# Attention and feed-forward layer in float32: maxima products moved into the middle of the background blocks

## What is computed

```python
scores = jnp.einsum('bhqd,bhkd->bhqk', Q, K) / np.sqrt(HD)
w = jax.nn.softmax(scores, axis=-1)
attn = jnp.einsum('bhqk,bhkd->bhqd', w, V)
x = _layernorm(x + (out @ Wo.T + bo))
g = jnp.einsum('th,ih->ti', xf, gate_w) * gate_s
u = jnp.einsum('th,ih->ti', xf, up_w) * up_s
out = jnp.einsum('ti,hi->th', jax.nn.silu(g) * u, down_w) * down_s
x = _layernorm(x + out)
```

## Time and profile before

| what | value |
|---|---|
| runs, median (lowest to highest) | 1011.74 us (1010.34 to 1012.72), 3 runs |
| profiled execution, device time | 1010.08 us |
| its span in the trace | 1008.1 us |
| PE, DVE, ACT busy | 99%, 80%, 64% of the span |
| granted TensorE clock | 0.998 |

### The profile page before, as it was taken

One profiled execution on the slowest core, in us unless ns is written; L12 is line 12 of the kernel. 1 busy time (PEld: TensorE's weight loads), 2 busy tenths in 40 slices (PEclk: granted clock), 3 DMA queues, 4 the chain that ended last, 5 costly groups with the idle time before them and its releaser, 6 DMA issues.

```text
span 1008.1 us, 17487 instructions
## 1 busy us (share of the span) xinstructions
PE 993.2 (99%) x6698; PEld 546.0 (54%) x6698; DVE 803.6 (80%) x1376; ACT 647.6 (64%) x1223; POOL 274.4 (27%) x284
## 2 busy tenths in 40 slices
PE   9999999999999999999999999999999999999996
PEld 4643435445434344443444444444368888888885
DVE  7999797998797999789899999999622666463635
ACT  5179796887787888788666688888852420322221
POOL 4361040241255540257210153565001001000002
PEclk9999999999999999999999999999999999999999
DMA  7174417234225531534140457331439113331011
GB/s 250 54 206 123 116 51 205 76 89 86 56 81 139 83 91 38 95 100 102 35 82 13 123 152 192 72 123 53 159 108 212 59 42 68 59 68 15 1 43 44
DMA packets 64297, 94.92 MB, mean 94 GB/s; under 512 B 37521, under 2 KB 37777, under 8 KB 62129
## 3 DMA queue, kind: packets, MB, share of 16 engines
q1 hardware_dynamic: 63920, 93.49, 36.5%
q10 hardware_dynamic: 288, 0.26, 0.1%
HBM read 53.88 MB, written 27.00 MB: 80 GB/s over the span
## 4 chain that ended last, share of the span: by engine, by line
PE 80%; DVE 15%; ACT 4%; issue 1%; DMA 1%; POOL 0%; DVEq 0%; POOLq 0%
PE PV L499 19%; PE PS L480 18%; PE PSA L570 16%; DVE nmx L1006 13%; PE PSA L458 6%; PE PS L587 6%; PE PS L402 4%; ACT Bn L802 3%; PE PS L526 2%; PE PSA L526 2%; PE PV L587 2%; PE PSA L402 1%; DVE nmx L1010 1%; PE PS L439 1%; DMA A<-in_wqk 1%
## 5 line engine op out<-in xcount | busy, mean ns | idle before, releaser
L1006 DVE TENSOR_REDUCE nmx<-PSA 128x1 f32<-128x512 f32 x976 | 592.6, 680 | 33.1 <-PE PSA L458 32.8
L802 ACT ACTIVATE Bn<-PS 128x512 f32<-128x512 f32 x898 | 476.5, 603 | 79.6 <-PE PS L480 72.5
L458 PE MATMUL PSA<-Kt,Qt 48*128 48x512 f32 x1010 | 359.7, 444 | 0.5 <-DVE nmx L1010 0.4
L480 PE MATMUL PS<-Qt,Kt 50*128 50x512 f32 x1006 | 341.8, 435 | 3.5 <-ACT Bn L802 3.0
L499 PE MATMUL PV<-Bn 128*32 128x256 f32 (+1 forms) x2696 | 298.0, 468 | 0.0
L480 PEld LDWEIGHTS PS<-Qt,Kt 50*128 50x128 f32 x1006 | 164.4, 184 | 240.8 <-ACT Bn L802 183.5
L458 PEld LDWEIGHTS PSA<-Kt,Qt 48*128 48x128 f32 x1010 | 165.7, 184 | 14.5 <-DVE nmx L1006 4.0
L570 PE MATMUL PSA<-x1Th,wr 128*128 128x512 f32 x344 | 135.3, 393 | 0.0
L570 PE MATMUL PSA<-x1Tl,wr 128*128 128x512 f32 x344 | 134.3, 390 | 0.0
L499 PE MATMUL PV<-P,Bn 128*32 128x512 f32 (+1 forms) x320 | 122.9, 466 | 0.0
L837 ACT ACTIVATE sg<-PSA,gs 128x512 f32<-128x512 f32 x43 | 29.6, 690 | 127.8 <-PE PSA L570 127.8
(11 more groups left out here) (177 smaller groups left out, 979.2 us busy)
## 6 DMA issues: line engine op xcount, KB each, us to landing
Qt<-pscr SPq DMA_DIRECT2D x90, 128.0 KB, 5.3
A<-in_wf SPq DMA_DIRECT2D x11, 768.0 KB, 5.5
wr<-A SPq DMA_DIRECT2D x33, 256.0 KB, 4.0
pscr<-A SPq DMA_DIRECT2D x16, 512.0 KB, 3.7
vscr<-Bn SPq DMA_DIRECT2D x32, 256.0 KB, 3.5
Kt<-pscr SPq DMA_DIRECT2D x90, 64.0 KB, 2.8
A<-A SPq DMA_DIRECT2D x16, 256.0 KB, 3.7
Bn<-vscr SPq DMA_DIRECT2D x8, 512.0 KB
```

Source lines behind the costliest of these rows:

```text
L458: op = e.matmul(slot_pair(s)[:, h, :], Qt[n % 3][p:p + NC_, g % 2, 128 * qt:128 * qt + 128], Kt[n % 3][p:p + NC_, 512 * h:512 * h + 512], ...
L480: e.matmul(score_tile(i), Kt[n % 3][rows, 128 * kt:128 * kt + 128], Qt[n % 3][rows, g % 2, 512 * qh:512 * qh + 512], start=True, stop=True ...
L802: e.activation(Pb[p_index(c)], score_tile(score_bank[c]), ACT.Exp, scale=0.25).then_inc(*act_exp.next(c))
L1006: e.tensor_reduce(col, slot_pair(s)[:, h, :], AX.X, ALU.max, negate=True).then_inc(*dve_max[s].next((k, 0) if h == 0 else k))
```

## The change

Four halves of the maxima stream (`AHEAD = 4`, two steps) are issued between the two banks of each of the 11 background blocks. In the four odd units behind a block, u + 1, u + 3, u + 5 and u + 7 (`paid_back`), the half behind the score g = 2 is left out, so that the stream is where it was at u + 8. On DVE, the units whose block has DVE work (42, 162, 170, 178, 186: `with_vector`) have two more `maximum` ahead of `first_norm`, `add_values` and `add_rows`, and units u + 3 and u + 7 behind them have one fewer (`taken_early`). In projection blocks DVE's order is as before. The total of products and reduces is unchanged.

```diff
--- before.py
+++ after.py
@@ -279,6 +279,11 @@
             ffn_at.setdefault(divmod((181, 184, 189, 192, 204, 205, 207, 209, 221, 223, 228)[i], 16), []).append(i)
             low_at.setdefault(divmod(180 + 8 * (1, 1, 2, 3, 4, 4, 5, 5, 6, 6, 7)[i], 16), []).append(i)
         before_flag = 508
+        AHEAD = 4
+        blocks = [16 * n + v for n, v in (*project_at, values_at, *out_at)]
+        paid_back = {b + 1 + 2 * i for b in blocks for i in range(AHEAD)}
+        with_vector = [16 * n + v for n, v in (values_at, *out_at)]
+        taken_early = {b + 4 * i + 3 for b in with_vector for i in range(AHEAD // 2)}
 
         crosswise = (0, 2, 1, 3)
 
@@ -501,8 +506,8 @@
                 if half != 0:
                     op.then_inc(*pe_pv.next(u))
 
-            def out_project(x, b, t2, banks, frees):
-                for j in range(2):
+            def out_project(x, b, t2, banks, frees, rows=(0, 1)):
+                for j in rows:
                     t = 2 * t2 + j
                     ps = banks[j]
                     clear(frees[j])
@@ -703,12 +708,19 @@
                 if at_u in project_at:
                     for h, i in enumerate(pair):
                         project_half(project_at[at_u], h, i, (0, 1, 2, 3))
+                        if h == 0:
+                            advance(AHEAD)
                 if at_u == values_at:
                     for t in range(8):
                         value_rows(1, t, pair[t // 4])
+                        if t == 3:
+                            advance(AHEAD)
                 if at_u in out_at:
                     t2 = out_at[at_u]
-                    out_project(False, 0, t2, [bank(i) for i in pair], [bank_free[i] for i in pair])
+                    for j, i in enumerate(pair):
+                        out_project(False, 0, t2, [bank(i) for i in pair], [bank_free[i] for i in pair], (j,))
+                        if j == 0:
+                            advance(AHEAD)
                     for j, i in enumerate(pair):
                         bank_free[i] = dve_y.at((False, 0, 2 * t2 + j))
 
@@ -716,7 +728,8 @@
                 at_u = divmod(u, 16)
                 for g in range(4):
                     scores(u, g)
-                    advance(1)
+                    if g != 2 or u not in paid_back:
+                        advance(1)
                     if g == 1:
                         background(u)
                     if u % 2 and u >= 2 and g == 0:
@@ -1278,7 +1291,10 @@
             for u in range(SPLIT):
                 at_u = divmod(u, 16)
                 maximum(next(steps))
-                k = next(steps)
+                if u in with_vector:
+                    maximum(next(steps))
+                    maximum(next(steps))
+                k = next(steps) if u not in taken_early else None
                 if at_u in norm_at:
                     first_norm(False, 0, norm_at[at_u])
                 if at_u == values_at:
@@ -1286,7 +1302,8 @@
                         add_values(1, h, i)
                 if at_u in out_at:
                     add_rows(False, 0, out_at[at_u], [bank(i) for i in free_banks(u)])
-                maximum(k)
+                if k is not None:
+                    maximum(k)
                 if at_u in recip_at:
                     reciprocal(recip_at[at_u])
                 if at_u == (15, 0):
```

## The result

The changed kernel takes 1057.38 us in the median (1048.98 to 1063.58, 4 runs) against 1011.78: a ratio of 1.045 (1.041 to 1.049). Slower, as forecast, but by 46 us instead of 26, and above the range's upper end of 1050.

A forecast was written before the change was run, and what follows sets the result against it. PE was taken to bound units with a block (0.57 us of waiting), DVE those without. Terms 9.7 + 12.7 - 6.3 + 10.8 = +26.9 us on 1010.1 made 1037.0; forecast 1037.5 us, range 1023 to 1050.

The forecast's parts named there:

- the price of the standstill: Behind blocks 170, 178 and 186 PE waits 3.6 us for add_rows, delayed by four reduces ahead of the norm: +10.8 us.
- the sentence that set the clock aside: On the page of the kernel before, PE's clock is granted in full in every slice, so it explains nothing; no size.
- Four halves in the block: Inside each of 11 blocks, four maxima products with no score beside them cost PE 0.88 us: +9.7 us.
- The collisions: From u + 2 to u + 7, shifted products share array halves with scores: 5 extra slots, 1.15 us a block, +12.7 us.
- Waits given back: In the eight units holding a block, PE's 0.57 us of waiting for DVE or ACT goes: -6.3 us.
- the sum: All terms over the 11 blocks together: +26.9 us on the profiled execution's 1010.1 us, making 1037.0.
- Rival 1: Where DVE sets the pace without a block, moved reduces come off its path: -17 us, 994 us; chance 4%.
- Rival 2: In PE's queue no product starts ahead of an earlier one: 10 slots instead of 5, 1050 us; chance 12%.
- Rival 3: Behind the blocks, shifted products fall into waits or overlap all the same: 12.7 us less, 1025 us; chance 10%.
- Rivals 4 and 5: 4: no standstill at the norm, 10.8 us less, 1027 us, chance 6%; 5: no change that can be told, 2%.

The follow-up runs named there:

- the first experiment: The changed kernel with the layer norm and first add_rows ahead of the extra reduces on DVE in units 170, 178 and 186; 1028.89 us, ratio 1.018.

## Why the prediction was wrong

**The step that failed** is the price of the standstill: "PE stands for 3.6 us ... 3 x 3.6 = +10.8 us", and, ahead of it, the sentence that set the clock aside as explaining nothing. The standstills came, three times, at the place, by the mechanism and with the length forecast (3.58 us each). But with each TensorE's clock also fell from 2.4 to 1.2 GHz (granted 1.00 to 0.50), at the latest 1.3 us behind PE's return. In the changed kernel's trace the clock was halved for 37.5, 10.2 and 10.2 us. Three runs show this from three sides: the standstill without the change makes it fall (0.981 to 0.989 in the mean); the change without the standstill doesn't (0.997 to 0.998); and the change with PE kept busy in the gap doesn't (0.997 to 0.998), and is 16 us faster than the same without. The Trainium skill (TensorE: Matmul & The Clock Gate, section HAM oscillation — how this bites in real kernels) names gaps in which PE is idle as what throttles it. The traces agree: each of their 13 standstills of 3.6 to 4.4 us comes with a fall, the three of 1.2 us with none. This rule belonged among the rivals, as it spoke against the change. With 16 us for the clock, the range would have had to reach some 1065.

The other terms, against their measurements:

- *Four halves in the block*, 0.88 us: measured 0.90. Right.
- *The collisions*, 5 slots and 1.15 us: 1.33 us in the mean of the 11 blocks. The number of slots is right: behind unit 162's block, in the first experiment's trace, the nine groups between two `weigh` have 3, 3, 4, 4, 2, 3, 4, 3 and 3 distinct starts, 5 more than three times 3, 2 and 3. What makes up the other 0.18 us was not looked into.
- *Waits given back*, 0.57 us: three pairs from u + 2 to u + 8 took 14.48 us in the mean of the 11 blocks before and take 13.90 with the collisions taken away, so 0.58. Right.
- A block costs 1.54 us in all in the first seven, where the sum had 1.46, and 2.0 in the three with a norm, their standstill not counted; the 11 make 18.2 in the first experiment's trace instead of 16.1.
- *The standstill itself*: 10.7 us instead of 10.8.
- The sum, which held nothing for the clock, gave 1037.0 for the profiled execution; the kernel that differs by the clock alone has 1041.46 there. Of these 4.5 us, 2.1 are the blocks', and 3.1 arise where nothing was moved (2.3 ahead of the first unit, 0.8 near unit 200); the 0.7 too many are spread over the other terms.

**The rivals.** Rival 1 (DVE's work taken off the path) is refuted for this form of the change: where all else is put right, 11 blocks end 0.4% above before (3.6 us of it theirs). Its mechanism exists, though: spread over 21 units in four blocks it makes the kernel 0.2% faster. Rival 2 (strict order of products) is refuted: a score passed three products, and the extra slots are 5. The Trainium skill's rule that products start in program order (TensorE: Matmul & The Clock Gate, section The mechanism, of Part 3) does not hold here for products on different halves of the array; the measurement decides. Rival 3 (collisions hidden) is refuted by the 13 us between the first experiment and the one with ordered heads. Rivals 4 and 5 didn't come.

## What to carry to other kernels

A wait of PE is worth its own length only if it is short. Here 1.2 us of standing still cost 1.2 us, while one of 3.6 to 4.4 us cost, by the medians, between 1.6 times (the kernel before with three of them) and 3.3 times (the changed kernel, measured again) its own length, as the clock fell with it. Where a wait of that length can't be avoided, products that nobody reads are cheaper than silence (16 us here); where it can, another order is cheaper still (28.5 us).

Where two streams share the array by halves, a change of one stream's phase costs a slot for each pair that no longer fits, and it can be counted from the code before any run (5 slots, 1.15 us, against 1.33 measured). Reordering the other stream to follow takes that cost away.

On an engine with a fixed order, work moved earlier must go behind whatever the other engines wait for next, and a lead is worth something only while it is being used up: four halves left out in one unit gave nothing, one by one they did.

## What was not expected of the hardware

- All 13 standstills in the five traces that have one, ten of 3.6 us and three of 4.4, came with a fall of the clock, between 1.9 us behind their start and 1.3 us behind their end; three of 1.2 us came with none. The mean clock of the executions without a trace (0.966 to 0.994) fits that. No run lies between 1.2 and 3.6 us.
- The clock also fell without one: for 3.4 us at 57 us in two traces, for 6.8 at 707 us in another, with no gap of PE over 0.6 us in the 50 us ahead. What made it fall there stays open.
- The half clock lasts for 3.4, 6.8, 10.2, 17.1 or 37.5 us in the traces here, behind standstills that are alike. Behind one and the same standstill of the changed kernel it lasted for 37.5 us in one trace and 6.8 in the other. The kernel varies by 17 us with it (1049 to 1066). Why the lengths differ stays open.
- Products on different halves of the array are started out of the queue's order, up to three places.
